# Bump attention: the key-query differences by TensorE in pairs of banks, one Abs over both, and a new order of the two lanes

## What is computed

```python
z_k = (x @ Wk.T + bk) @ Wproj.T     # one number per token and head, keys
z_q = (x @ Wq.T + bq) @ Wproj.T     # the same for the queries
out_i = sum_j max(0, 1 - |zq_i - zk_j| / b_h) * v_j / T      # for every head h
```

## Time and profile before

| | us |
|---|---|
| median of three runs | 1359.96 |
| lowest, highest | 1358.13, 1365.36 |
| span of the profiled execution | 1360.6 |
| busy in it: TensorE | 1153.6 |
| VectorE | 761.6 |
| ScalarE | 657.0 |
| GpSimd | 339.0 |

### The profile page before, as it was taken

One profiled execution on the slowest core, in us unless ns is written; L12 is line 12 of the kernel. 1 busy time (PEld: TensorE's weight loads), 2 busy tenths in 40 slices (PEclk: granted clock), 3 DMA queues, 4 the chain that ended last, 5 costly groups with the idle time before them and its releaser, 6 DMA issues.

```text
span 1360.6 us, 19642 instructions
## 1 busy us (share of the span) xinstructions
PE 1153.6 (85%) x7254; PEld 651.8 (48%) x7254; DVE 761.6 (56%) x1977; ACT 657.0 (48%) x1132; POOL 339.0 (25%) x735
## 2 busy tenths in 40 slices
PE   7949577789789999979997867778879999988986
PEld 6934321353344567744465431333334467764455
DVE  4654685557595421278345577577587332159443
ACT  2116279615238643316743549844317743323861
POOL 3032210233335200034503121042424300032520
PEclk9759578759699999989998967788779989989998
DMA  7040000120430000070024100021330000033011
GB/s 248 1 109 14 10 1 1 38 73 7 106 91 3 4 1 1 1 186 3 3 63 114 34 1 1 3 69 39 98 98 4 3 2 1 0 113 75 3 42 37
DMA packets 48348, 57.85 MB, mean 43 GB/s; under 512 B 16469, under 2 KB 41349, under 8 KB 47750
## 3 DMA queue, kind: packets, MB, share of 16 engines
q1 hardware_dynamic: 47390, 56.13, 15.3%
q10 hardware_dynamic: 864, 0.48, 0.1%
HBM read 35.13 MB, written 20.87 MB: 41 GB/s over the span
## 4 chain that ended last, share of the span: by engine, by line
PE 63%; DVE 20%; ACT 10%; POOL 3%; issue 3%; DMA 2%; SPq 0%; ACTq 0%; POOLq 0%; DVEq 0%
PE banks L1616 10%; PE banks L1606 10%; ACT sb_arena L1299 6%; PE banks L1422 5%; PE banks L1410 5%; DVE sb_rmax L1551 5%; PE banks L1397 3%; PE banks L957 2%; PE banks L470 2%; PE banks L1249 2%; PE banks L605 2%; PE banks L1275 2%; PE banks L465 2%; POOL sb_rstd L461 1%; PE banks L675 1%
## 5 line engine op out<-in xcount | busy, mean ns | idle before, releaser
L1551 DVE TENSOR_REDUCE sb_rmax<-banks 128x1 f32<-128x384 f32 (+3 forms) x352 | 204.8, 637 | 73.8 <-PE banks L1399 73.4
L1480 ACT ACTIVATE sb_arena<-banks 128x512 f32<-128x512 f32 x320 | 175.2, 597 | 94.6 <-PE banks L1410 93.7
L1299 ACT ACTIVATE sb_arena<-banks,sb_zk 128x512 f32<-128x512 f32 x256 | 152.7, 821 | 22.2 <-PE banks L1249 20.9
L1397 PE MATMUL banks<-sb_arena,sb_qs 128*128 128x128 bf16 (+3 forms) x512 | 131.0, 325 | 25.2 <-DVE sb_rmax L1551 19.6
L1671 ACT ACTIVATE sb_arena<-banks,sb_b 128x512 f32<-128x512 f32 x128 | 87.3, 687 | 132.9 <-PE banks L1606 131.6
L460 POOL TENSOR_SCALAR sb_var<-sb_mv 128x4 f32<-128x4 f32 x40 | 10.3, 258 | 562.0 <-DVE sb_mv L445 561.9
L1616 PEld LDWEIGHTS banks<-sb_w,sb_arena 128*128 128x128 f32 x1024 | 126.4, 193 | 32.7 <-issue 32.7
L1509 POOL TENSOR_SCALAR_AFFINE_SELECT sb_arena<-sb_arena 128x256 f32<-128x256 f32 x256 | 99.1, 408 | 172.2 <-ACT sb_arena L1480 172.2
L1730 DVE SCALAR_TENSOR_TENSOR sb_xall<-banks,sb_region,sb_xall 128x128 f32<-128x128 f32 x160 | 44.9, 344 | 157.8 <-PE banks L1616 157.8
L1616 PE MATMUL banks<-sb_w,sb_arena 128*128 128x128 f32 x1024 | 127.1, 276 | 0.0
L1606 PE MATMUL banks<-sb_ft,sb_w 128*128 128x512 f32 x256 | 126.6, 607 | 0.0
(11 more groups left out here) (281 smaller groups left out, 1888.0 us busy)
## 6 DMA issues: line engine op xcount, KB each, us to landing
sb_qs<-q_scratch SPq DMA_DIRECT2D x32, 288.0 KB, 4.8
q_scratch<-sb_region SPq DMA_DIRECT2D x16, 384.0 KB, 2.5
sb_arena<-k_scratch SPq DMA_DIRECT2D x16, 288.0 KB, 6.9
sb_arena<-in_chosen SPq DMA_DIRECT2D x8, 514.0 KB, 4.3
sb_w<-in_w SPq DMA_DIRECT2D x2, 2048.0 KB
q_scratch<-sb_region SPq DMA_DIRECT2D x16, 256.0 KB, 2.1
sb_qs<-q_scratch SPq DMA_DIRECT2D x32, 96.0 KB, 2.3
k_scratch<-sb_region SPq DMA_DIRECT2D x8, 384.0 KB, 2.6
```

What stands on the lines that cost most here:

```text
L1299: i = nc.scalar.activation(L.dist[h % 3][:, kb, :], (b2_, b3)[h % 2], ACT.Abs, bias=L.zk[:, kb, h:h + 1])
L1397: nc.tensor.matmul(o[:, i * kl:(i + 1) * kl], L.qs[:, h // 2, t * 128:kl], L.ks[:, key_of(h), 0:kl], start=(i == 0), stop=False)
L1480: nc.scalar.activation(L.probs[:, u % SLOTS, :], bank_of(SELF_ORDER, ring, ("key", u)), ACT.Exp)\
L1551: nc.vector.tensor_reduce(L.rmax[:, t, g * GROUP + h0:g * GROUP + h0 + nh], bank_of(SELF_ORDER, ring, ("max", step))[:, 0:nh * kl] .rearra ...
```

## The change

1. Differences by TensorE. The folded weights `wz` become one 128x128 matrix, whose product has, in each group of 32 rows, the 16 z_q and the 16 z_k. One bias for both. VectorE splits all 128 rows in three parts (rows 0 to 31 the first, 32 to 63 the second, 64 to 95 the third), then makes, with `zmask` as scale and offset, four forms for the queries (`L.zquery`, one for each group of four heads) and four for the keys (`L.zkey`, one for each place in a group), 128 rows of bf16 each, in the memory of `L.qs`. A matmul of one key block of `zkey` with `zquery` gives z_q - z_k of one head and 128 keys. `differences(h, half)` writes two key blocks, in b2 and b3; it waits for the Abs of the half before.
2. One Abs over both banks (`L.pair`, 128x1024), without a bias; two a head in place of four.
3. The values are waited for only before the first weighted values. `L.zk`, the key projection, the selector `sel` and GpSimd's memset of `L.zpart` go. Stage W folds both projections and the bias with two accumulating matmuls each.
4. `L.mrows` and its selector grow from 12 to 128 rows, of which the other 116 are zero (set once by GpSimd at the start).
5. Some first `yield`s move, and all `ORDER` strings are new.

```diff
-    "SP":
-    "2fa516bc1ff006fe01ac5fc06a67fe422f01ff801fe01ac5fc06a648",
+    "SP":
+    "3baa16c5f7d005fe016cfd405667fe4218bee7401fe0159d7c05a6508",
...
+        self.pair = psum[:, 4 * u + 2:4 * u + 4, :]
...
-        self.zpart = self.k32[0:96, 0:256].bitcast(BF16)
-        self.zmid = self.k32[0:H, 256:512].bitcast(BF16)
+        self.zpart = self.k32[:, 0:256].bitcast(BF16)
+        self.zmid = self.k32[:, 256:512].bitcast(BF16)
+        zrows = self.qs32[:].bitcast(BF16).rearrange("p (s g n) -> p s g n", s=2, g=GROUP)
+        self.zquery, self.zkey = zrows[:, 0], zrows[:, 1]
...
-        self.mrows = sb(f"mrows{u}", [3 * GROUP, 2, S], BF16)
+        self.mrows = sb(f"mrows{u}", [128, 2, S], BF16)
...
-                                 mselb[:, h % GROUP:h % GROUP + 1].to_broadcast([3 * GROUP, 128]),
+                                 mselb[:, h % GROUP:h % GROUP + 1].to_broadcast([128, 128]),
                                  L.mrows[:, h // GROUP % 2, :], start=False, stop=True, skip_group_check=True)\
...
-            nc.tensor.matmul(b2_[0:H, :], wz[:, 1, :], L.ft[:], start=True, stop=True).then_inc(L.sem("q"), 1)
-            project_tokens(b3, L.ft, wz[:, 0, :], H).then_inc(L.sem("k"), 1)
+            nc.tensor.matmul(b2_, wz[:], L.ft[:], start=True, stop=True).then_inc(L.sem("q"), 1)
             yield
             project_tokens(b1_, L.ft, weight("b_v")).then_inc(L.sem("v"), 1)
 
-            def spread(h):
-                if h >= 2:
-                    pe.wait_ge(*p.at("dist", h - 1))
-                nc.tensor.matmul((b2_, b3)[h % 2], selb[:, h:h + 1].to_broadcast([96, 128]), L.zpart,
-                                 start=True, stop=True).then_inc(L.sem("spread"), 1)
+            def differences(h, half):
+                g, j = h // GROUP, h % GROUP
+                if half == 0 and (g == 0 or j == 0):
+                    pe.wait_ge(*p.at("zrows", GROUP + 1 + g if g else j + 2))
+                if h or half:
+                    pe.wait_ge(*p.at("dist", 2 * h + half))
+                for n in range(2):
+                    kb = 2 * half + n
+                    i = nc.tensor.matmul((b2_, b3)[n], L.zkey[:, j, kb * 128:(kb + 1) * 128], L.zquery[:, g, :],
+                                         start=True, stop=True)
+                i.then_inc(L.sem("diff"), 1)
...
-            yield
-            pe.wait_ge(*p.at("q_split", 1))
-            pe.wait_ge(*p.at("k32", 1))
-            pe.wait_ge(*p.at("values", 1))
-            spread(0)
-            spread(1)
             for h in range(H):
-                yield
-                if h + 2 < H:
-                    spread(h + 2)
+                for half in range(2):
+                    yield
+                    differences(h, half)
                 if h:
                     yield
+                    if h == 1:
+                        pe.wait_ge(*p.at("values", 1))
                     weighted_values(h - 1)
...
-                act.wait_ge(*p.at("spread", h + 1))
-                if h >= 3:
-                    act.wait_ge(*p.at("pv", h - 2))
-                for kb in range(T):
-                    i = nc.scalar.activation(L.dist[h % 3][:, kb, :], (b2_, b3)[h % 2], ACT.Abs,
-                                             bias=L.zk[:, kb, h:h + 1])
-                i.then_inc(L.sem("dist"), 1)
+                for half in range(2):
+                    yield
+                    act.wait_ge(*p.at("diff", 2 * h + half + 1))
+                    if h >= 3 and half == 0:
+                        act.wait_ge(*p.at("pv", h - 2))
+                    nc.scalar.activation(L.dist[h % 3][:, 2 * half:2 * half + 2, :], L.pair, ACT.Abs)\
+                        .then_inc(L.sem("dist"), 1)
...
-            nc.gpsimd.memset(L.zpart, 0.0)
             nc.gpsimd.memset(L.bumps, 0.0).then_inc(L.sem("filled"), 1)
...
+            dve_chain(nc.vector.tensor_copy(L.zpart, L.q32[:]))
+            dve_chain(nc.vector.tensor_tensor(L.zres, L.q32[:], L.zpart, ALU.subtract))
+            dve_chain(nc.vector.tensor_copy(L.zmid, L.zres))
+            nc.vector.tensor_copy(L.zpart[32:64, :], L.zmid[32:64, :])
+            nc.vector.tensor_tensor(L.zpart[64:96, :], L.zres[64:96, :], L.zmid[64:96, :], ALU.subtract)\
+                .then_inc(L.sem("q_split"), 1)
+
+            def z_rows(dst, side, n):
+                nc.vector.tensor_scalar(dst[:, n, :], L.zpart, zmask[:, side, n, 0:1], zmask[:, side, n, 1:2],
+                                        ALU.mult, ALU.add).then_inc(L.sem("zrows"), 1)
+
+            yield
+            dve.wait_ge(*p.at("q_split", 1))
+            z_rows(L.zquery, 0, 0)
+            z_rows(L.zkey, 1, 0)
+            yield
+            for j in range(1, GROUP):
+                z_rows(L.zkey, 1, j)
+            yield
+            for g in range(1, G):
+                z_rows(L.zquery, 0, g)
```

More of the change, by code:

```diff
@@ L156 @@
            "down_picked": 1, "down": 1, "hid": 1, "filled": 1, "up_picked": 1, "y": 1, "res": 1},
-    "BU": {**_LN, "turned": 1, "ft": 1, "k": 1, "k32": 1, "q": 1, "q32": 1, "q_split": 1, "v": 1, "values": 1,
-           "filled": 1, "spread": H, "dist": H, "hat": H, "pv": H, "osb": G, "y": 1, "res": 1},
+    "BU": {**_LN, "turned": 1, "ft": 1, "q": 1, "q32": 1, "q_split": 1, "zrows": 2 * G, "v": 1, "values": 1,
+           "filled": 1, "diff": 2 * H, "dist": 2 * H, "hat": H, "pv": H, "osb": G, "y": 1, "res": 1},
     "S0": {**_SELF, "k_edged": EDGES, "x5": 1},
@@ L194 @@
+    "f843b2a0",
 }
@@ L280, in __init__ @@
         self.mparts = sb(f"mparts{u}", [128, 2, T, 2, 3, GROUP // 2], BF16)
-        self.mrows = sb(f"mrows{u}", [3 * GROUP, 2, S], BF16)
+        self.mrows = sb(f"mrows{u}", [128, 2, S], BF16)
         self.sums = sb(f"sums{u}", [128, T, H])
-        self.zk = sb(f"zk{u}", [128, T, H])
         self.zsum = sb(f"zsum{u}", [128, 4])
@@ L1285, in bump_scalar @@
             act.wait_ge(*p.at("q", 1))
-            nc.scalar.activation(L.q32[0:H, :], b2_[0:H, :], ACT.Identity, bias=zqbias[:, 0:1]).then_inc(L.sem("q32"), 1)
+            nc.scalar.activation(L.q32[:], b2_, ACT.Identity, bias=zbias[:, 0:1]).then_inc(L.sem("q32"), 1)
             def keep(g):
@@ L1435, in self_tensor @@
             for step in range(SELF_STEPS):
-                yield
+                if step:
+                    yield
                 if step == NM:
@@ L1806, in _ @@
                     nc.gpsimd.memset(lane.cks32[:], 0.0)
+                    nc.gpsimd.memset(lane.mrows[:], 0.0)
                     nc.gpsimd.memset(lane.qs32[:], 0.0)
@@ L1863, in lay_out @@
     late = (-BIG * (key > query)).astype(np.float32)
-    sel = np.zeros((96, H), np.float32)
-    msel = np.zeros((3 * GROUP, GROUP), np.float32)
+    zmask = np.zeros((4, 2, G, GROUP, 2, GROUP, 2), np.float32)
+    for n in range(GROUP):
+        zmask[:3, 0, n, :, 0, n, 0] = 1
+        zmask[:3, 1, n, :, 0, n, 1] = 1
+        zmask[:3, 1, :, n, 1, n, 0] = -1
+        zmask[:3, 0, :, n, 1, n, 1] = 1
+    wproj = np.zeros((D, 2, 4, 2, H), np.float32)
+    for side in range(2):
+        wproj[:, side, :, side, :] = t(i["L1_attn_Wproj"])[:, None, :]
+    msel = np.zeros((128, GROUP), np.float32)
     for part in range(3):
-        sel[part * 32:part * 32 + H] = np.eye(H)
         for j in range(GROUP):
```

106 lines of the change are left out of this document (43 added, 63 removed).

## The result

The changed kernel takes **1381.6 us** (median of 4, 1377.0 to 1383.1) against 1359.8 for the kernel before in the same comparison; the ratio is 1.015, 95% interval 1.0115 to 1.0185. Forecast was 1356, range 1335 to 1378. The profiled execution took 1383.1 us with a span of 1381.3 (before: 1360.6).

What follows compares the result with a forecast made beforehand. ScalarE was taken to bound the bump with both lanes in it, one lane's chain elsewhere in that loop. Bump rounds -3 and +6, rows -4, rest of the order -3 sum to -4: 1356 us, range 1335 to 1378.

Steps and rivals of the forecast that it cites:

- the rest of the new order: Shorter waits in X0, F0 and W from the new order strings: -3 us.
- the bump rounds: Bump attention loops with their lane exits: -3 us in round 1, +6 us carried for round 2.
- The Abs: Bump's Abs over two banks: 1.03 us alone, 0.93 in a row, saving 29 us of ScalarE in 64 heads.
- it does not do what it says: Rival: reading two banks costs as much as two pieces, ScalarE again the bound, +10, 1368 us; chance 0.06.
- The pair of differences and the single lane: Bump with one lane: pair 0.60 us, half 1.70, head 3.4 warm; tails at 3.75 a head.
- Two lanes in the loop: Bump with both lanes: 4.1 us for two heads, bounds 3.9 and 4.6, TensorE over 90% busy.
- Handover as the slower rival: Rival: Abs and differences taking turns on one pair of banks cost +22, giving 1378 us; chance 0.24.
- Place of the lanes: Lane 0 enters the bump after 5.5 heads of lane 1, first Abs at 197.5 and 828 us.
- F0 gets freer: Lane 0's expert stage on VectorE, no longer cut by lane 1's bump instructions: 3 to 9 us freer.
- The stages lie against each other as before everywhere: Order outside the bump rounds: claimed unchanged between the stages of both lanes.
- The rows: Maxima matmul in X1 at 128 rows: -4 us by a higher clock, from bounds of 0 to 23.
- what would show it wrong: Signs against the forecast, among them over 5 us difference between the traces outside the bump and X1 stages.

Runs made afterwards that it cites:

- e4: The kernel before with only the maxima's rows raised from 12 to 128; 1348.3 us, ratio 0.9898.
- e13: The old bump code with 128 rows for the maxima, in the order of e2; 1367.7 us, ratio 1.0065.
- e2: The changed kernel with the old interleaving from lane 0's S0 of round 1 to its X0 of round 2, on all engines; 1365.8 us, ratio 1.0039.
- e1: The changed kernel with a separate Abs for each bank of differences, four a head, each matmul waiting only for its own bank; 1373.2 us, ratio 1.0100.
- e6: e1 with the weighted values sent one head later on TensorE; 1372.4 us, ratio 1.0072.
- e3: The changed kernel with the maxima matmul back at 12 rows; 1406.6 us, ratio 1.0345.
- e14: The changed kernel with the old interleaving on SP alone, from lane 0's S0 of round 1 to its X0 of round 2; 1375.2 us, ratio 1.0116.
- e15: The changed kernel with the old interleaving in the stretch of e14 on every engine but SP; 1374.9 us, ratio 1.0099.
- e11_spread128: e4 with the rows of the bump's spread matmul also raised from 96 to 128; 1348.2 us, ratio 0.9911.

## Why the prediction missed, step by step

The changed kernel was slower by 1.5% where no change or a small gain was forecast, and above the range. The parts can be added up from the runs, each with the uncertainty said above. Before to e4: rows, -13.9. e4 to e13: new order around the bumps, +22.7. e13 to e2: new bump code, -3.5. e2 to the change: new order in the middle, +15.1. Sum +20.4. The prediction had -4 for the rows, -3 for "the rest of the new order", and -3 and +6 for the bump rounds: -4. The two steps that failed are the place of the lanes around the bump, put at -3 and +6, and the order between the bumps, put at nothing but a small gain.

- **The Abs**, right: 1.026 us alone against 1.03. By the Trainium skill ("ScalarE: Activation LUTs", section "What ACT_TABLE_LOAD costs") 186 ns + 1024 x 0.833 ns give an estimate of 1.039; the trace agrees within 1.3%. The 0.93 in a row was right too: where pieces of both lanes follow each other they start 0.90 to 0.92 apart, 21 times between 200 and 242. One lane's own pieces never stand in a row, which the wait of differences(h, half) could have told. The rival "it does not do what it says" is out (its 1368 should read 1366: +10 on 1356).
- **The pair of differences and the single lane**, right in mechanism: 0.60 us and 1.72 a half against 0.60 and 1.70. The tails were taken at 3.75 a head and came at 4.0 once lane 1's end was through (round 1 from 253.0 to 272.8, round 2 from lane 0's ninth head at 898.7 to its last at 927.0). As wholes they were mis-sized more, 30.0 and 41.7 us where 24.4 and 33.8 stood: the folds of lane 1, booked only as a gain for lane 1, stand in lane 0's way.
- **Two lanes in the loop**, mis-sized: 4.1 us forecast for two heads, 4.54 measured, TensorE 83% busy where over 90% was expected, though the clock of 1.00 was right. I had added up one engine's work and allowed 0.2 for the turns; e1 shows that a second bank returns part of the difference (4.36).
- **Handover as the slower rival** (1378), near the time by luck and wrong on the cause. e1 and e6 price it at 7 and 9 us, not 22. Its main row was misread: the 93.2 us of the earlier trace rows add the idle time of the weight load (66.8) and of the matmul (26.4), which overlap; TensorE's matmuls waited 26.4 us for an Abs before and 36.0 after. The Trainium skill ("PSUM — Partial Sum Buffer", "Summary: rules for kernel authors") spoke for this rival; e1 and e6 agree with its rule in sign. Without the rows' gain the kernel would have been at 1406.6 (e3), beyond every case that I had.
- **Place of the lanes**, failed. "F0 gets freer" was right (24.3 us for 28.3), and so was lane 0's start after 5.5 heads. What I did not ask is what the uncut F0 delays: lane 1's hat by 8 us, and by the F0 matmul in TensorE's queue lane 1's differences. Lane 0's first Abs, forecast at 197.5 and 828, came at 199.2 and 844.7; of the 17 us in round 2, 13.5 were lost before X0 ended. Round 1's bump ended 1.0 us later, where -3 was forecast. From the end of X0 to the end of lane 0's bump round 2 took 14.7 us more in e2 (130.4) than in e4 (115.7), where +6 stood, and e13, with the old code, 17.3 more (133.0).
- **"The stages lie against each other as before everywhere"**, failed, the largest error after the one above. I compared the order at the level of stages; inside them it had changed, and 15 us hang on it, by e2; the traces of e14 and e15 each lose some of the waits for late transfers. The last line of "what would show it wrong" named it: over 5 us between the traces outside the bump and X1.
- **The rows**, right in sign, mis-sized: 4 us, taken at the low end of 0 to 23, were 13.9 on the kernel before and 26.5 on the changed one. The row's duration at equal clock (0.39 both) says nothing of what it does to the clock.

What stays open: which places of the order around the bumps carry the 22.7 us. The hole of lane 1 (some 7 us beyond its usual 4) and the folds are seen, but no run takes one of them away alone. The two traces differ by 13.0 us only, e4's being of its slowest execution, and they part in round 2's F0 and bump (17.3 us, of which some comes back behind it). The best of these versions is e4_rows128_alone, at 1348.3 us, with e11_spread128 level with it.

## What to carry to other kernels

An order of instructions that was fitted to one set of durations is a part of the kernel with a price of its own: change the code and the order in separate runs, for here the two together hid a gain of 14 us and a loss of about 38. When an interleaving is redrawn, follow each transfer's issue and each engine's longest uninterrupted piece against the other lane's waits, not the stages as wholes. A loop of one lane in which two engines take turns on one buffer costs the sum of both (here 1.02 + 0.70 us a half), not the larger, however cheap either has become.

## What the runs showed of the hardware

More rows in a matmul raised the granted clock in X1, although the added rows held nothing but zeros. X1's 16 matmuls a round and lane with 12 rows and 512 columns take about the same 0.38 us at the 2.4 GHz level as with 128 rows. But with 128 rows in the kernel before X1 is granted 0.80 and 0.82 (288 to 362, 909 to 978) in place of 0.77 in both rounds, and in the change 0.80 and 0.88 in place of 0.59 and 0.72. 64 rows give about half of the time of 128, with 0.77 and 0.81 (286 to 363, 909 to 983). The Trainium skill ("TensorE: Matmul & The Clock Gate", "Part 1: The HAM clock gate") has the clock set by how busy the engine has been; in e3 and the change TensorE has the same instructions in the same order, and the clock still differs with the rows of this one matmul. In the bump, with 128 rows in place of 96, the picture is mixed (0.84 in place of 0.72 with one lane, 0.80 in place of 0.86 with two), and nothing came of it in time.
